# Expert feed-forward: tokens sorted by expert into 16 full tiles instead of 23 padded ones

## The chip, the cores and the metric

One core of a Trainium2 chip runs the whole kernel. The metric is device time in microseconds (us). Three runs of the kernel before took 903.69 to 904.23 us, median 903.89.

## The reference, cut to what matters

Two attention blocks come first (relative-bias attention over 2 x 1024 tokens of 128 features, then a second attention over the same tokens). The change touches only the last block, a mixture of experts in which every token goes to exactly one of 8 experts:

```python
def _moe_mlp(x, gate_w, gate_b, w1, w2):
    xf = x.reshape(b * n, d)                       # 2048 tokens x 128
    logits = xf @ gate_w + gate_b                  # 8 experts
    one_hot = jax.nn.one_hot(jnp.argmax(logits, axis=-1), E, dtype=xf.dtype)
    h = jax.nn.gelu(jnp.einsum('td,edh->teh', xf, w1), approximate=True)   # 128 -> 512
    y = jnp.einsum('teh,ehd->ted', h, w2)                                  # 512 -> 128
    out = jnp.einsum('te,ted->td', one_hot, y)
    return out.reshape(b, n, d)
...
x = x + _moe_mlp(_layernorm(x, ln2_w, ln2_b), gate_w, gate_b, w1, w2)
```

A layer norm of the result is then added to the residual stream.

## The kernel before

Everything until about 805 us of the span is attention, and the change leaves it alone. What follows, in the order of the program:

- **Gate and plan.** VectorE (DVE) picks each token's expert (L1121 to L1134). TensorE (PE) counts, by matmuls over the one-hot matrix, each token's rank within its expert and each expert's total (L1468 to L1473). From these DVE works out a slot for every token (L1140 to L1158). Each expert begins at a fresh tile of 128 slots, so that up to NS = (T - E) // 128 + E = 23 tiles can be needed for T = 2048 tokens, and 23 are always run. Two numbers per token, multiplied by PE with a matrix of places (L1477), are turned into the list of tokens per slot: `gather_u` for reading, `token_u` for writing (empty slots write into a spare region of `moe_out`), and `expert_u`, the expert of each tile (L1163 to L1175). These small steps follow one another through `chain`, which waits for each to end.
- **Gather.** GpSimd (POOL) issues 23 indirect DMAs that read 128 token rows each from `tokens` in DRAM (L797). The rows have been stored there by one DMA per half of the tokens (L556).
- **Tile loop.** For tile j, PE transposes the rows (`sorted_rows`, L1486), DVE applies scale and shift of the layer norm on the way out of PSUM (`features`, L1195), PE multiplies by the expert's first weights (`up`, 8 recorded matmuls, L1494), ScalarE (ACT) applies GELU (L942), PE multiplies by the second weights (`down`, L1503), and DVE copies the result to `slot_y` (`result`, L1188). The weights of the tile's expert are copied by DVE from `w_moe` into one of four buffers (`weights`, L1184). Which expert it is stands in SBUF, so a `value_load` (L1181) brings it into a register of DVE first. PE's order per step is transpose of j+1, up of j, down of j-1, and DVE's is features of j+1, weights of j+2, result of j-1.
- **Scatter.** After its 23 gathers POOL issues 23 indirect DMAs that write the result rows to `moe_out` (L803), each when its tile's result is there.
- **End.** When all have landed, SP loads `moe_out` back in token order (L613), and DVE, POOL and ACT add, normalise, add the residual and store.

The loops of DVE and PE, and POOL's list:

```python
for j in range(NS):                       # DVE, L1201
    if j + 1 < NS: features(j + 1)
    if j + 2 < NS: weights(j + 2)
    if j: result(j - 1)
...
for j in range(NS):                       # PE, L1508
    if j + 1 < NS: sorted_rows(j + 1)
    up(j)
    if j: down(j - 1)
...
for j in range(NS):                       # POOL, L801
    pool.wait_ge(y_ready, j + 1)
    ...
```

## Time and profile before

| | |
|---|---|
| median of 3 runs | 903.89 us (903.69 to 904.23) |
| the profiled execution, its own time | 904.78 us |
| its span in the profile | 902.4 us |
| busy: PE, DVE, ACT, POOL | 802.4, 751.3, 636.4, 242.4 us |
| mean granted clock of PE | 0.948 of full speed |

The profile gives, for one execution, busy times of the engines, groups of instructions by line, and the chain of waits that ended last. Times of rows are microseconds from the start of the span. A row of a timeline has the start, the duration, the engine, the line, the operation, what it writes and reads, and in brackets how long the engine sat idle before it and what ended that. A name with q (DVEq, SPq) is the sequencer of the engine, which handles register loads, register arithmetic and DMA issues and runs ahead of the engine itself. "issue" means that the engine waited for nothing that the profile shows. The groups of rows below come from these views.

### The profile page before, as it was taken

The numbers are of one execution on the slowest core, as the hardware profiler recorded it, in microseconds if no ns is written. First come the engines' busy times: TensorE is split into PE (matmuls) and PEld (weight loads), VectorE is DVE, ScalarE is ACT, GpSimd is POOL, SyncE is SP. The second block draws the span as 40 slices with busy tenths as digits, with TensorE's granted clock in tenths as the row PEclk, the third lists the DMA queues.
The fourth block names the chain that finished last, engine by engine and source line by source line (L and its number), as shares of the span: only waits on it lengthen the run. The fifth ranks groups of instructions, "written<-read, shape, count | busy, mean of one in ns | idle before, by whom it ended". The sixth has DMA issues, their size and how long they took to land.

```text
span 902.4 us, 24156 instructions
## 1 busy us (share of the span) xinstructions
PE 802.4 (89%) x9661; PEld 308.1 (34%) x9661; DVE 751.3 (83%) x1195; ACT 636.4 (71%) x1267; POOL 242.4 (27%) x548
## 2 busy tenths in 40 slices
PE   5279999999999999999999999999999999955950
PEld 3013334333333333343333223322332322344950
DVE  4489988999999998889999998899999999236634
ACT  5037777777776777777778989999989999921311
POOL 3110413200000415232300543332011401004773
PEclk9559999999999999999999999999999999976985
DMA  3665444555555455346313333332321221101313
GB/s 88 185 194 176 144 138 161 170 177 172 171 176 175 137 165 171 117 158 202 108 50 110 107 112 101 102 92 76 93 66 55 61 81 53 31 16 50 51 53 99
DMA packets 69476, 104.78 MB, mean 116 GB/s; under 512 B 15845, under 2 KB 45861, under 8 KB 69365
## 3 DMA queue, kind: packets, MB, share of 16 engines
q1 hardware_dynamic: 62773, 68.30, 26.5%
q10 hardware_dynamic: 5120, 31.94, 9.9%
q0 software_dynamic: 1472, 3.02, 1.6%
q8 instruction: 76, 1.25, 0.6%
q14 instruction: 35, 0.29, 0.1%
HBM read 84.19 MB, written 18.87 MB: 114 GB/s over the span
## 4 chain that ended last, share of the span: by engine, by line
PE 69%; DVE 9%; POOL 6%; issue 4%; DMA 4%; ACT 4%; SPq 3%; POOLq 0%; DVEq 0%
PE bank L1304 23%; PE bank L1323 21%; PE bank L1330 12%; PE bank L1284 7%; DVE unit_max L1013 4%; ACT prob_mem L907 4%; POOL prob_mem L797 3%; POOL moe_out L803 2%; PE bank L1249 1%; DVE stats L956 1%; PE bank L1371 1%; DMA maxima_rows<-max_rows 1%; PE bank L1257 1%; DMA k_parts<-prob_mem 1%; DMA bias_parts<-prob_mem 1%
## 5 line engine op out<-in xcount | busy, mean ns | idle before, releaser
L907 ACT ACTIVATE prob_mem<-bank 128x512 f32<-128x512 f32 x1024 | 556.6, 597 | 137.8 <-PE bank L1330 115.1
L1284 PE MATMUL bank<-k_rows,q_rows 56*128 56x512 bf16 x1024 | 328.2, 392 | 22.2 <-DMA k_rows<-k_parts 12.7
L1323 PE MATMUL bank<-q_rows,k_rows 59*128 59x512 bf16 x1024 | 334.4, 385 | 5.4 <-DMA q_rows<-maxima_rows 1.9
L1009 DVE CUSTOM_DVE_ANT_1 no_use<-bank,w_moe 128x1024 bf16<-128x1024 f32 x256 | 305.6, 1219 | 30.8 <-PE bank L1284 27.7
L1304 PE MATMUL bank<-prob_mem,v_ring 128*32 128x256 f32 x4096 | 320.4, 386 | 7.8 <-issue 6.7
L1013 DVE TENSOR_REDUCE unit_max<-bank 128x1 f32<-128x1024 f32 x256 | 297.4, 1217 | 15.0 <-PE bank L1284 13.4
L1323 PEld LDWEIGHTS bank<-q_rows,k_rows 59*128 59x128 bf16 x1024 | 81.1, 93 | 243.2 <-ACT prob_mem L907 117.9
L708 POOL CAST max_parts<-unit_max 128x8 bf16<-128x8 f32 x64 | 12.1, 189 | 553.3 <-DVE unit_max L1009 312.8
L1304 PEld LDWEIGHTS bank<-prob_mem,v_ring 128*32 128x32 f32 x4096 | 102.6, 109 | 153.6 <-ACT prob_mem L907 60.5
L1330 PE MATMUL bank<-skew_mem,pick 96*32 96x512 bf16 x1664 | 138.3, 390 | 0.0
L1284 PEld LDWEIGHTS bank<-k_rows,q_rows 56*128 56x128 bf16 x1024 | 77.1, 93 | 32.7 <-DVE unit_max L1009 14.7
L1020 DVE TENSOR_TENSOR bank<-bank,w_moe 128x512 f32<-128x512 f32 x96 | 67.0, 698 | 23.1 <-PE bank L1323 23.0
L1330 PEld LDWEIGHTS bank<-skew_mem,pick 96*32 96x32 bf16 x1664 | 29.1, 94 | 71.2 <-issue 71.2
L942 ACT ACTIVATE prob_mem<-bank 128x512 f32<-128x512 f32 x23 | 13.7, 598 | 39.1 <-PE bank L1494 37.8
L859 ACT COPY max_rows<-bank 24x128 bf16<-24x128 bf16 x64 | 15.8, 247 | 24.2 <-PE bank L1313 24.2
L797 POOL DMA_INDIRECT prob_mem<-tokens,gather_u x23 | 23.9, 1037 | 19.5 <-DVE gather_u L1166 12.8
L1494 PE MATMUL bank<-prob_mem 128*128 128x128 f32 x184 | 26.0, 288 | 0.0
L803 POOL DMA_INDIRECT moe_out<-prob_mem,token_u x23 | 23.4, 1019 | 7.0 <-issue 7.0
L852 ACT COPY o_ring<-bank 128x256 f32<-128x256 f32 x64 | 24.3, 380 | 1.2 <-PE bank L1304 1.2
L1503 PE MATMUL bank<-prob_mem 128*128 128x128 f32 x184 | 24.3, 276 | 0.0
L1494 PEld LDWEIGHTS bank<-prob_mem 128*128 128x128 f32 x184 | 24.1, 204 | 0.0
L1024 DVE RECIPROCAL recip<-bank 128x128 f32<-128x128 f32 (+1 forms) x5 | 4.0, 792 | 22.9 <-PE bank L1336 22.9
(181 smaller groups left out, 532.2 us busy)
## 6 DMA issues: line engine op xcount, KB each, us to landing
w_moe<-bias_rows ACTq DMA_DIRECT2D x31, 960.0 KB, 5.8
q_rows<-q_parts SPq DMA_DIRECT2D x252, 48.0 KB
k_rows<-k_parts SPq DMA_DIRECT2D x126, 96.0 KB
skew_mem<-bias_parts SPq DMA_DIRECT2D x32, 378.0 KB, 4.1
unit_sums<-o_ring SPq DMA_DIRECT2D x63, 128.0 KB, 2.3
w_moe<-in_L_ffn_w_dram SPq DMA_DIRECT2D x16, 256.0 KB, 3.0
q_parts<-prob_mem SPq DMA_DIRECT2D x8, 384.0 KB, 3.1
k_parts<-prob_mem SPq DMA_DIRECT2D x24, 128.0 KB, 2.7
```

What stands on the lines that cost most here:

```text
L797: nc.gpsimd.indirect_dma_start(out=slot_rows[:, j, :], out_offset=None, in_=tokens_dram, in_offset=bass.IndirectOffsetOnAxis(ap=gather_u[: ...
L803: nc.gpsimd.indirect_dma_start(out=moe_dram, out_offset=bass.IndirectOffsetOnAxis(ap=token_u[:, j:j + 1], axis=0), in_=slot_y[:, j, :], in ...
L852: nc.scalar.copy(o_ring[:, n % 2, :], AV).then_inc(o_ready, 1)
L907: nc.scalar.activation(prob[:, kb, half * N:(half + 1) * N], b_bank(("exp", exp_no(n, kb, half))), ACT.Exp).then_inc(exp_done, 1)
L1009: nc.vector.tensor_tensor_reduce(out=no_use[:, qb % 2, :].rearrange("p (k c) -> p k c", k=QB), in0=scores.rearrange("p (k c) -> p k c", k= ...
L1013: nc.vector.tensor_reduce(unit_max[:, m % 2, qb:qb + 1], scores, AX.X, ALU.max).then_inc(max_done, 1)
L1020: nc.vector.tensor_tensor(half, half, bias_tab[:, n % 4, at:at + N], ALU.add).then_inc(bias_added, 1)
L1284: return nc.tensor.matmul(sa_slot(QB * m + qb)[:, f, :], q_rows[rows, m % SLOTS, qb * P:(qb + 1) * P], k_rows[rows, m % SLOTS, f * N:(f + ...
L1304: ins = nc.tensor.matmul(AV[VM * c:VM * (c + 1), :], v_ring[:, n % 4, kb, :], prob[:, kb, c * W:(c + 1) * W], start=(kb == 0), stop=(kb == ...
L1323: return nc.tensor.matmul(b_bank(("exp", exp_no(n, kb, f))), k_rows[rows, n % SLOTS, kb * P:(kb + 1) * P], q_rows[rows, n % SLOTS, f * N:( ...
L1330: ins = nc.tensor.matmul(b_bank(("exp", exp_no(n, kb, f)))[32 * c:32 * (c + 1), :], pick[:], skew[0:96, n % 3, at:at + N], start=False, st ...
L1494: ins = nc.tensor.matmul(bank[:, 2 + j % 2, c * P:(c + 1) * P], w_ring[:, j % 4, c * P:(c + 1) * P], slot_feat[:, j % 4, :], start=True, s ...
```

## The change

The tokens are sorted by expert without gaps, so that 16 tiles hold all of them. A tile then may hold tokens of several experts: the tile loop runs over 23 pairs of one tile and one expert (16 tiles and at most 7 borders between experts). For each pair the whole tile goes through the expert, and the result is added to the tile's row of `slot_y` under a mask `in_pair` that is 1 for the rows of that expert. `slot_y` is zeroed first by POOL. Gathers and scatters are 16 each. The scatter of tile j waits for j + 8 results, or for all 23. Scale and shift of the layer norm move to ACT (`tile_features`), once per tile, into `tile_feat`; `features(j)` on DVE is now a copy from the pair's tile, whose number comes by a `value_load` of `tile_u`. So does the row of `slot_y` in `result(j)`.

The diff, cut to its core (declarations, renamed sizes and the repeated NS to TT replacements are left out):

```diff
             store_tokens(1, LN_TAIL)
-            sp.wait_ge(y_scattered, 16 * NS)
+            sp.wait_ge(y_scattered, 16 * TT)
             moe_tiles = moe_dram[0:T].rearrange("(t p) d -> p t d", p=P)
             for g in range(G):
...
@@ -792,14 +800,14 @@
             pool.wait_ge(tokens_stored, 16 * B)
-            pool.wait_ge(gather_known, 1)
-            for j in range(NS):
+            nc.gpsimd.memset(slot_y[:], 0.0).then_inc(y_zeroed, 1)
+            pool.wait_ge(tokens_known, 1)
+            for j in range(TT):
                 nc.gpsimd.indirect_dma_start(out=slot_rows[:, j, :], out_offset=None, in_=tokens_dram,
-                                             in_offset=bass.IndirectOffsetOnAxis(ap=gather_u[:, j:j + 1], axis=0)
+                                             in_offset=bass.IndirectOffsetOnAxis(ap=token_u[:, j:j + 1], axis=0)
                                              ).then_inc(slots_loaded[arrival(j)[0]], 16)
-            pool.wait_ge(tokens_known, 1)
-            for j in range(NS):
-                pool.wait_ge(y_ready, j + 1)
+            for j in range(TT):
+                pool.wait_ge(y_ready, min(j + E, NS))
                 nc.gpsimd.indirect_dma_start(out=moe_dram, out_offset=bass.IndirectOffsetOnAxis(ap=token_u[:, j:j + 1], axis=0),
                                              in_=slot_y[:, j, :], in_offset=None).then_inc(y_scattered, 16)
             for g in range(1, G, 2):
@@ -935,7 +943,15 @@
             act.wait_ge(gate_step, AT_LEAST_STEP)
             nc.scalar.activation(numbers[:, :, 0, :], at_least[:], ACT.Identity, scale=row_no[:, 0:1]).then_inc(numbers_ready, 1)
+            def tile_features(t):
+                act.wait_ge(slot_t_mm, t + 1)
+                nc.scalar.activation(tile_feat[:, t, :], bank[:, t % 2, 0:P], ACT.Identity, scale=ln_par[:, 2:3],
+                                     bias=ln_par[:, 3:4]).then_inc(feat_ready, 1)
+
+            tile_features(0)
             for j in range(NS):
+                if j + 1 < TT:
+                    tile_features(j + 1)
                 act.wait_ge(up_mm, j + 1)
                 if j >= 2:
                     act.wait_ge(down_mm, j - 1)
@@ -1137,43 +1153,38 @@
             dve.wait_ge(rank_mm, 1)
             rank = bank[:, 6, 0:(TT + 1) * E].rearrange("p (t e) -> p t e", e=E)
-            chain(nc.vector.tensor_copy(end_tile[:], rank[:, TT, :].rearrange("p (e o) -> p e o", o=1)))
-            chain(nc.vector.tensor_tensor(counts[:], spread_ap(end_tile[:, :, :], [1, E], [0, TT]),
-                                          spread_ap(tile_start[:, :], [0, E], [1, TT]), ALU.is_gt))
-            chain(nc.vector.tensor_reduce(tiles_of[:], counts[:], AX.X, ALU.add))
-            chain(nc.vector.tensor_tensor(pairs_ef[:], lower[:], spread_ap(tiles_of[:, :, :], [0, E], [1, E]), ALU.mult))
-            chain(nc.vector.tensor_reduce(first_tile[:], pairs_ef[:], AX.X, ALU.add))
-
-            chain(nc.vector.scalar_tensor_tensor(place[:], spread_ap(first_tile[:, :, :], [0, TT], [1, E]), float(P),
-                                                 rank[:, 0:TT, :], ALU.mult, ALU.add))
+            chain(nc.vector.tensor_copy(expert_count[:], rank[:, TT, :].rearrange("p (e o) -> p e o", o=1)))
+            chain(nc.vector.tensor_tensor(pairs_ef[:], lower[:], spread_ap(expert_count[:, :, :], [0, E], [1, E]), ALU.mult))
+            chain(nc.vector.tensor_reduce(first_slot[:], pairs_ef[:], AX.X, ALU.add))
+            chain(nc.vector.tensor_tensor(place[:], spread_ap(first_slot[:, :, :], [0, TT], [1, E]), rank[:, 0:TT, :], ALU.add))
             chain(nc.vector.tensor_tensor(place[:], place[:], hot, ALU.mult))
             chain(nc.vector.tensor_reduce(slot_f[:], place[:], AX.X, ALU.add))
-            slot_by_tile = spread_ap(slot_f[:, :], [1, TT], [0, NS + 1])
-            chain(nc.vector.tensor_tensor(at_least[:], slot_by_tile, spread_ap(tile_start[:, :], [0, TT], [1, NS + 1]), ALU.is_ge))
-            chain(nc.vector.tensor_reduce(slot_tile[:], at_least[:, :, 1:NS + 1], AX.X, ALU.add))
+            slot_by_tile = spread_ap(slot_f[:, :], [1, TT], [0, TT + 1])
+            chain(nc.vector.tensor_tensor(at_least[:], slot_by_tile, spread_ap(tile_start[:, :], [0, TT], [1, TT + 1]), ALU.is_ge))
+            chain(nc.vector.tensor_reduce(slot_tile[:], at_least[:, :, 1:TT + 1], AX.X, ALU.add))
             chain(nc.vector.scalar_tensor_tensor(place_in_tile[:], slot_tile[:], -float(P), slot_f[:], ALU.mult, ALU.add))
             nc.vector.tensor_tensor(has_place, spread_ap(col_no[:, :], [0, TT], [1, P]),
                                     spread_ap(place_in_tile[:, :], [1, TT], [0, P]), ALU.is_equal).then_inc(numbers_ready, 1)
-            nc.vector.tensor_tensor(numbers[:, :, 1, :], at_least[:], spread_ap(next_tile_no[:, :], [1, TT], [0, NS + 1]),
+            nc.vector.tensor_tensor(numbers[:, :, 1, :], at_least[:], spread_ap(next_tile_no[:, :], [1, TT], [0, TT + 1]),
                                     ALU.mult).then_inc(numbers_ready, 1)
+            chain(nc.vector.tensor_tensor(counts[:], spread_ap(first_slot[:, :, :], [1, E], [0, TT]),
+                                          spread_ap(tile_start[:, :], [0, E], [1, TT]), ALU.is_ge))
+            chain(nc.vector.tensor_reduce(tiles_of[:], counts[:], AX.X, ALU.add))
             dve.wait_ge(numbers_mm, 1)
-            chain(nc.vector.tensor_copy(slot_sum[:], bank[:, 7, 0:NS + 1]))
-            chain(nc.vector.scalar_tensor_tensor(slot_sum[:], bank[:, 7, NS + 1:2 * NS + 2], float(P), slot_sum[:], ALU.mult, ALU.add))
-            chain(nc.vector.tensor_tensor(slot_token[:], slot_sum[:, 0:NS], slot_sum[:, 1:NS + 1], ALU.subtract))
-            nc.vector.tensor_scalar(gather_u[:], slot_token[:], -float(P), 0.0, ALU.add, ALU.max).then_inc(gather_known, 1)
-            chain(nc.vector.scalar_tensor_tensor(unused[:], slot_token[:], 0.0, spare_no[:], ALU.is_le, ALU.mult))
-            nc.vector.scalar_tensor_tensor(token_u[:], slot_token[:], -float(P), unused[:], ALU.add, ALU.add).then_inc(tokens_known, 1)
-
-            chain(nc.vector.tensor_tensor(end_tile[:], first_tile[:], tiles_of[:], ALU.add))
-            chain(nc.vector.tensor_tensor(ended[:], spread_ap(end_tile[:, :, :], [0, NS], [1, E]),
-                                          spread_ap(tile_no[:, :], [1, NS], [0, E]), ALU.is_le))
+            chain(nc.vector.tensor_copy(slot_sum[:], bank[:, 7, 0:TT + 1]))
+            chain(nc.vector.scalar_tensor_tensor(slot_sum[:], bank[:, 7, TT + 1:2 * TT + 2], float(P), slot_sum[:], ALU.mult, ALU.add))
+            chain(nc.vector.tensor_tensor(slot_token[:], slot_sum[:, 0:TT], slot_sum[:, 1:TT + 1], ALU.subtract))
+            nc.vector.tensor_scalar(token_u[:], slot_token[:], -float(P), None, ALU.add).then_inc(tokens_known, 1)
+
+            chain(nc.vector.tensor_tensor(ended[:], spread_ap(tiles_of[:, :, :], [0, NS], [1, E]), turn_no[:], ALU.is_le))
             chain(nc.vector.tensor_reduce(expert_f[:], ended[:], AX.X, ALU.add))
-            chain(nc.vector.tensor_scalar(expert_f[:], expert_f[:], float(E - 1), None, ALU.min))
-            nc.vector.tensor_copy(expert_u[:], expert_f[:]).then_inc(expert_known, 1)
-            dve.wait_ge(expert_known, 1)
+            nc.vector.tensor_scalar(expert_u[:], expert_f[:], -1.0, None, ALU.add).then_inc(expert_known, 1)
+            chain(nc.vector.tensor_tensor(tile_f[:], pair_no[:], expert_f[:], ALU.subtract))
+            nc.vector.tensor_copy(tile_u[:], tile_f[:]).then_inc(expert_known, 1)
+            dve.wait_ge(expert_known, 2)
             dve.wait_ge(moe_loaded, 16 * 2 * E)
             def weights(j):
@@ -1184,20 +1195,36 @@
                 nc.vector.tensor_copy(w_ring[:, j % 4, :], w_moe[:, bass.ds(e, 1), :].rearrange("p o w -> p (o w)")).then_inc(w_ready, 1)
             def result(j):
+                tile = dve.value_load(tile_u[0:1, j:j + 1], min_val=0, max_val=TT - 1)
                 dve.wait_ge(down_mm, j + 1)
-                nc.vector.tensor_copy(slot_y[:, j, :], bank[:, 4 + j % 2, 0:D]).then_inc(y_ready, 1)
+                if j:
+                    dve.wait_ge(y_ready, j)
+                rows = slot_y[:, bass.ds(tile, 1), :].rearrange("p o d -> p (o d)")
+                nc.vector.scalar_tensor_tensor(rows, bank[:, 4 + j % 2, 0:D], in_pair[:, j:j + 1], rows, ALU.mult,
+                                               ALU.add).then_inc(y_ready, 1)
             def features(j):
-                dve.wait_ge(slot_t_mm, j + 1)
+                tile = dve.value_load(tile_u[0:1, j:j + 1], min_val=0, max_val=TT - 1)
+                dve.wait_ge(feat_ready, min(j, TT - 1) + 1)
                 if j >= 4:
                     dve.wait_ge(up_mm, j - 3)
-                nc.vector.tensor_scalar(slot_feat[:, j % 4, :], bank[:, j % 2, 0:P], ln_par[:, 2:3], ln_par[:, 3:4],
-                                        ALU.mult, ALU.add).then_inc(slot_t_ready, 1)
+                nc.vector.tensor_copy(slot_feat[:, j % 4, :], tile_feat[:, bass.ds(tile, 1), :].rearrange("p o n -> p (o n)")
+                                      ).then_inc(slot_t_ready, 1)
             weights(0)
             weights(1)
             features(0)
+
+            chain(nc.vector.tensor_tensor(ended[:], ended[:], spread_ap(first_slot[:, :, :], [0, NS], [1, E]), ALU.mult))
+            chain(nc.vector.tensor_reduce(pair_start[:, 0:NS], ended[:], AX.X, ALU.max))
+            chain(nc.vector.scalar_tensor_tensor(pair_start[:, 0:NS], tile_f[:], float(P), pair_start[:, 0:NS], ALU.mult, ALU.max))
+            chain(nc.vector.tensor_scalar(pair_slot[:], tile_f[:], float(P), row_no[:, 0:1], ALU.mult, ALU.add))
+            chain(nc.vector.tensor_tensor(from_next[:], pair_slot[:], pair_start[:, 1:NS + 1], ALU.is_ge))
+            chain(nc.vector.tensor_tensor(in_pair[:], pair_slot[:], pair_start[:, 0:NS], ALU.is_ge))
+            chain(nc.vector.tensor_tensor(in_pair[:], in_pair[:], from_next[:], ALU.subtract))
+            dve.wait_ge(y_zeroed, 1)
+
             for j in range(NS):
                 if j + 1 < NS:
                     features(j + 1)
...
@@ -1482,7 +1509,7 @@
                 pe.wait_ge(slots_loaded[arrival(j)[0]], 16 * arrival(j)[1])
                 if j >= 2:
-                    pe.wait_ge(slot_t_ready, j - 1)
+                    pe.wait_ge(feat_ready, j - 1)
                 nc.tensor.transpose(bank[:, j % 2, 0:P], slot_rows[:, j, :], ident[:]).then_inc(slot_t_mm, 1)
             def up(j):
@@ -1506,7 +1533,7 @@
             sorted_rows(0)
             for j in range(NS):
-                if j + 1 < NS:
+                if j + 1 < TT:
                     sorted_rows(j + 1)
                 up(j)
                 if j:
```

On DVE one step of the tile loop read as follows before (the loop of L1201; `expert_u` is the list of experts, L1184 the copy of the weights, L1188 the result, L1195 the features):

```order
L1181 TENSOR_LOAD expert_u
L1181 ISA x2
L1184 ISA [waits down_mm]
L1184 COPY prob_mem<-w_moe 128x1024
L1188 COPY prob_mem<-bank 128x128 [waits down_mm]
L1195 TENSOR_SCALAR prob_mem<-bank,ln_par 128x128 [waits up_mm,slot_t_mm]
```

and now so (`tile_u` is the list of tiles; L1195 is now the copy of the weights, L1203 the result, L1212 the features):

```order
L1192 TENSOR_LOAD expert_u
L1192 ISA x2
L1195 ISA [waits down_mm]
L1195 COPY prob_mem<-w_moe 128x1024
L1198 TENSOR_LOAD tile_u
L1198 ISA x2
L1203 ISA [waits y_ready,down_mm]
L1203 SCALAR_TENSOR_TENSOR prob_mem<-bank,in_pair,prob_mem 128x128
L1208 TENSOR_LOAD tile_u
L1208 ISA x2
L1212 ISA [waits up_mm,feat_ready]
L1212 COPY prob_mem<-prob_mem 128x128
```

Each of the three instructions of a step now has its own register load and register arithmetic ahead of it, where one of three had before.

Between the first features and the second, DVE now works out the masks:

```order
L1212 COPY prob_mem<-prob_mem 128x128
L1219 TENSOR_TENSOR ended<-ended,first_slot 128x184
L1220 TENSOR_REDUCE pair_start<-ended 128x23 [waits gate_step]
L1221 SCALAR_TENSOR_TENSOR pair_start<-tile_f,pair_start 128x23 [waits gate_step]
L1222 TENSOR_SCALAR pair_slot<-tile_f,row_no 128x23 [waits gate_step]
L1223 TENSOR_TENSOR from_next<-pair_slot,pair_start 128x23 [waits gate_step]
L1224 TENSOR_TENSOR in_pair<-pair_slot,pair_start 128x23 [waits gate_step]
L1225 TENSOR_TENSOR in_pair<-in_pair,from_next 128x23 [waits gate_step]
L1208 TENSOR_LOAD tile_u [waits y_zeroed,gate_step]
L1208 ISA x2
L1212 ISA [waits feat_ready]
```

Seven chained steps now stand there, where nothing stood before; the second features come behind them.

On ACT the table load of GELU stood right behind `numbers`, and now stands behind the features of two tiles (L948):

```order
L944 ACTIVATE numbers<-prob_mem,row_no 128x16x17 [waits gate_step]
L948 ACTIVATE prob_mem<-bank,ln_par 128x128 [waits slot_t_mm] x2
L958 ACT_TABLE_LOAD
L958 ACTIVATE prob_mem<-bank 128x512 [waits up_mm]
L948 ACTIVATE prob_mem<-bank,ln_par 128x128 [waits slot_t_mm]
```

The table load moved past two waits for PE's transposes.

## Rows read from the trace of the kernel before

**Rows 1.** Busy time of each engine by stretch (PE, PEld, DVE, ACT, POOL, PEclk, DMA, GB/s).

```profile
840.00:850.00 10.00, 10.00 (x92) 10.00 (x91) 6.93 (x16) 3.21 (x6) 7.72 (x8) 1.00 0.30 46
...
870.00:880.00 10.00, 0.43 (x4) 0.24 (x3) 0.29 (x1) 0.00 (x0) 7.56 (x9) 0.66 0.16 52
```

**Rows 2.** Timeline of POOL, first gather, first and last scatter.

```profile
820.63 1.24 POOL L797 DMA_INDIRECT prob_mem<-tokens,gather_u  x1 [12.75 <-DVE gather_u L1166]
...
851.49 1.01 POOL L803 DMA_INDIRECT moe_out<-prob_mem,token_u  x1 [0.30 <-issue]
...
880.66 0.97 POOL L803 DMA_INDIRECT moe_out<-prob_mem,token_u  x1 [0.30 <-issue]
```

**Rows 3.** Timeline of PE, start of the tile loop and one step of it.

```profile
824.72 0.47 PE L1486 MATMUL bank<-ident,prob_mem 128*128 128x128 f32 x1 [0.77 <-DMA prob_mem<-tokens,gather_u]
824.99 1.92 PE L1494 MATMUL bank<-prob_mem 128*128 128x128 f32 x8
...
829.72 1.06 PE L1494 MATMUL bank<-prob_mem 128*128 128x128 f32 x8
...
831.62 1.06 PE L1494 MATMUL bank<-prob_mem 128*128 128x128 f32 x8
```

**Rows 4.** Timeline of DVE in the tile loop, and its last result.

```profile
825.24 0.41 DVE L1195 TENSOR_SCALAR prob_mem<-bank,ln_par 128x128 f32<-128x128 f32 x1 [0.83 <-PE bank L1486]
825.97 0.69 DVE L1184 COPY prob_mem<-w_moe 128x1024 f32 x1 [0.32 <-issue]
...
829.81 0.29 DVE L1188 COPY prob_mem<-bank 128x128 f32<-128x128 f32 x1 [1.23 <-PE bank L1503]
830.02 0.40 DVE L1195 TENSOR_SCALAR prob_mem<-bank,ln_par 128x128 f32<-128x128 f32 x1
830.68 0.69 DVE L1184 COPY prob_mem<-w_moe 128x1024 f32 x1 [0.25 <-issue]
...
870.47 0.29 DVE L1188 COPY prob_mem<-bank 128x128 f32<-128x128 f32 x1 [0.66 <-PE bank L1503]
```

**Rows 5.** Instructions of lines L1181 and L1184 in DVE's sequencer (min/median/max ns).

```profile
L1181 DVEq TENSOR_LOAD <-expert_u x23: 301/304/550, 821.4 to 864.1; - x23
L1181 DVEq FUSED_REGOPS  x23: 190/190/207, 821.9 to 864.4; - x23
...
L1184 DVEq FUSED_REGOPS  x23: 57/57/65, 822.2 to 864.7; - x23
```

**Rows 6.** Timeline of DVE in the plan, and the first two copies of weights.

```profile
811.74 0.29 DVE L1141 TENSOR_TENSOR counts<-end_tile,tile_start 128x128 f32<-128x128 f32 x1
...
813.87 0.56 DVE L1153 TENSOR_TENSOR prob_mem<-slot_f,tile_start 128x384 f32<-128x384 f32 x1
...
819.57 0.18 DVE L1166 TENSOR_SCALAR gather_u<-slot_token 128x23 uint32<-128x23 f32 x1
...
820.16 0.35 DVE L1171 TENSOR_TENSOR ended<-end_tile,tile_no 128x184 f32<-128x184 f32 x1
...
822.36 1.44 DVE L1184 COPY prob_mem<-w_moe 128x1024 f32 x2 [1.04 <-issue]
```

**Rows 7.** Groups of instructions by line: a memset of POOL, a copy of ACT.

```profile
L676 POOL MEMSET v_ring<- 128x1024 f32 x1 | 1.0, 951 | 0.0
...
L852 ACT COPY o_ring<-bank 128x256 f32<-128x256 f32 x64 | 24.3, 380 | 1.2 <-PE bank L1304 1.2
```

**Rows 8.** Second store of the tokens on SP; DMA issues (KB each, us to landing).

```profile
811.39 0.40 SPq L556 DMA_DIRECT2D tokens<-norm  x1
...
tokens<-norm SPq DMA_DIRECT2D x2, 512.0 KB, 3.2
```

**Rows 9.** Busy time of PE by stretch (PE busy, PEclk, DMA, GB/s).

```profile
600.00:620.00 20.00, 18.67 (x202) 1.00 0.37 101
...
790.00:795.00 5.00, 1.07 (x16) 0.97 0.17 49
795.00:800.00 5.00, 4.63 (x23) 0.50 0.00 0
```

50 lines of the change are left out of this document (29 added, 21 removed).

## The prediction

> **What bounds the kernel now.** I read the busy times by stretch first, for the part behind 820 us. At 840 to 850 us both PE and POOL are at work all the time (POOL shows 7.72 of 10 us, the rest being the issue gaps between its DMAs), and at 870 to 880 us POOL alone still works [rows 1]. The timeline of POOL says what this is. The first gather begins at 820.63 us, the first scatter at 851.49 and the last of 23 scatters at 880.66, with nothing but 0.30 us of issue ahead of each [rows 2]. So 23 gathers take 30.9 us, 1.34 us each, and the scatters stand (880.66 - 851.49) / 22 = 1.33 us apart. The timelines of the two other engines show that they have finished long before. One step of the tile loop takes PE 831.62 - 829.72 = 1.90 us [rows 3], and DVE's last result is there at 870.47 + 0.29 = 870.8 us [rows 4]. The end of the span hangs on POOL's list, which is 10 us late against the last result. Everything behind the last scatter waits for it and isn't changed.
>
> **What the change does, part by part.**
>
> *POOL's list* loses 14 of 46 DMAs, 14 x 1.33 = 18.7 us. Only a part of it can be had, since the tile loop still has 23 steps and the last scatter needs the last result. The question is when that result comes.
>
> *The plan* ahead of the gathers gets shorter. Two operations on 128 elements per partition leave the chain (the one whose row stands there takes 0.29 us and, with the gap behind it, 0.32), and come back behind `numbers`, where DVE waits for PE anyway: 0.64 us. Three operations of 384 elements become 272 wide. Between 128 elements (0.29 us) and 384 (0.56 us) one element costs 1.05 ns, so each gives 0.12 us: 0.36. Together the token list is known 1.0 us earlier, and the first gather begins at 819.6 instead of 820.63; it begins 0.9 us behind the end of the instruction that makes the list, 819.57 + 0.18 [rows 2, 6]. The list of experts loses three small operations and gains two, so it comes about 1.2 us earlier, ahead of need.
>
> *The memset on POOL* is new: twice the size of one that took 0.95 us, so 1.9 us [rows 7]. The tokens' store is issued at 811.39 us and lands 3.2 us behind its issue of 0.4 us [rows 8], at 815.0. The memset is over at 816.9, and POOL waits for the token list until 818.8. It costs nothing; uncovered it would cost at most its 1.9 us.
>
> *The start of the loop.* PE's first `up` waited for the second gather (its transpose at 824.72, `up` at 824.99) [rows 3], so it begins at 824.0. Features now go PE, ACT, DVE. On ACT a copy of 256 elements from PSUM takes 0.38 us [rows 7], so 0.3 for 128; this lies under the wait for the second gather. ACT's table load stands now behind two of these, between them and the first GELU, and that GELU waits for `up(0)`, which takes 1.92 us at the clock of that time [rows 3]. I cost it at nothing, with 0.3 us as its upper bound.
>
> *The masks* are seven chained operations on DVE between the first features and the second. Two are 184 wide, 0.35 us and a gap [rows 6], the others 23 wide at some 0.21 from start to start (the 0.18 of the 23-wide row and a gap). That makes 2 x 0.38 + 5 x 0.21 = 1.8 us. With the first features done at 823.7 they end at 825.5. A register load that follows such a chain took 1.04 us from the last operation to the copy [rows 6], so the second features start at 826.5 and `up(1)` at 826.75. Before it was 824.99 + 1.92 = 826.9. **The microsecond won in the plan is lost again.** Bounds: 0.8 us of the 1.04 if its load had been a fast one, which would leave a gain of 0.4.
>
> *DVE's step* decides. One step had one register load, now it has three. In DVE's sequencer a load takes 0.304 us, the register arithmetic behind it 0.19 and 0.057 [rows 5]. From the start of an instruction to the start of one with a load ahead of it it is 825.97 - 825.24 = 0.73 us, and 830.68 - 830.02 = 0.66 where the earlier one had been handed over before its engine was free [rows 4]. The sequencer runs ahead: two copies of weights, the second with its own load, take 1.44 us together, thus 0.72 each and hardly more than the copy's own 0.69 [rows 6, 4]. So a load hides behind the instruction ahead of it, but not behind another load. Three of them give a step of 3 x 0.72 = 2.16 us on DVE, where PE needs 1.90. The work itself hides in it: 0.69 for weights, under 0.4 for a copy of features and some 0.3 for the result. **The loop changes from PE-bound to DVE-bound.** Bounds for one load: 0.55 (the sequencer's own parts, where nothing else cost anything; PE's 1.90 then holds) and 0.80 (0.73 and a gap of 0.07 for the additional wait in `result`).
>
> *The sum.* `result(0)` comes at 829.9, as before (829.81) [rows 4], since the low clock holds PE back there. `result(19)` follows 19 x 2.16 = 41.0 us later, at 870.9. Features of step 22 follow 0.7 later, at 871.6 and done at 871.8. Then PE has `up(22)`, `down(21)`, `down(22)`, each half of 1.90: 874.65. The result is written by 875.0. POOL's gathers end at 819.6 + 16 x 1.34 = 841.1; its scatter j waits for result j + 7, which come 2.16 us apart against 1.33 for a scatter, so POOL waits for each, and the last goes out right behind the last result. With the 0.9 us that POOL took from the token list to its first gather it starts at 875.9, where it was 880.66 [rows 2]. **That is 4.8 us less.** The profiled execution, 904.78, becomes 900.0. It lies 0.9 above the median of 903.89, which becomes **899.1**. With the bounds of one load, 0.01 us on each of 57 loads is 0.57 us: 0.80 gives 903.7, and the lower bound the first rival below.
>
> About 0.2% (1.8 us) is what a measurement of this kernel can tell from no change.
>
> **The rivals.**
>
> 1. *The loop stays PE-bound.* Loads overlap with each other's arithmetic or cost less than 0.63 each, so a step stays at 1.90. Then the last result comes as before less 0.15, is written at 870.6, and the last scatter starts at 871.5: 9.2 us less, 894.7. For it speaks that the sequencer's own parts sum to 0.55 us [rows 5]; against it that no pair of rows is closer than 0.66. I give it 0.17.
>
> 2. *Loads are dearer than that, and the kernel gets slower.* A DVE step above (4.8 / 19) + 2.16 = 2.41 us, or 0.80 a load, takes the gain away. One of the 23 loads took 0.55 us instead of 0.304 [rows 5]. If all did, a step would be 3 x (0.72 + 0.25) = 2.9 us and the time 899.1 + 19 x 0.74 = 913. Against it: 0.304 is the median of 23, and the slow one is the first, behind a wait. 0.07.
> The Trainium skill, "DMA: Bandwidth & Descriptors", section "Latency and other measured facts", gives such a load a floor of about 600 ns. By that rule a step would be above 3 us and the kernel slower by more than 10 us; the trace's 0.304 us disagrees, and I go by the trace.
>
> 3. *PE's clock falls.* In a DVE-bound loop PE stands still for 0.26 of 2.16 us in each step, 12%. At the low clock `up` takes 1.92 us instead of 0.95 [rows 3], a step 3.9, that is 1.7 us more than DVE's; three such steps take the gain, ten make it 911. Against it: PE was 93% busy at 600 to 620 us and had full clock throughout; the clock fell only behind a stretch with PE busy for 1.07 of 5 us [rows 9]. 88% is much nearer to the first. 0.04.
> The Trainium skill, "TensorE: Matmul & The Clock Gate", section "A second HAM failure mode: psum-queue depth-cycling", describes a kernel in which micro-idles between groups of matmuls made the clock oscillate; by that rule this rival would be the outcome. No row here shows small idles doing it.
>
> 4. *The gain drowns.* Twice as many sequencer instructions in the loop, fetched late a few times, and a load price near 0.78 leave less than 1.8 us. 0.10.
>
> **How the numbers follow.** DVE-bound as summed 0.62, PE-bound 0.17, drowned 0.10, dear loads 0.07, clock 0.04. The likeliest gives 899.1, with 896.5 to 902 as its own range. To hold 8 in 10 the range must take in the PE-bound case at 894.7, with the 0.4 us that the masks may leave and as much for the start of the loop, and reach to the upper bound of the load: 893.9 to 903.7. Faster by over 0.2% is the first two, 0.79, and no more; within 0.2% 0.11 and slower 0.10.
>
> **What would show it.** Right: in the timeline of DVE the starts of `result` stand 2.1 to 2.25 us apart, with idle "issue" time ahead of each instruction and none put down to PE; PE shows gaps of 0.2 to 0.3 us in each step that end with the features; the first gather begins at 819.6, the first scatter waits for DVE, and the last starts within 1 us of the last result, near 876 us. A second `up` before 826.3 or after 827.2 makes the price of the masks wrong. Results 1.90 us apart speak for rival 1, above 2.4 for rival 2; a granted clock below 1.00 between 832 and 870 us for rival 3. The whole argument is wrong if the last scatter starts later than 1.5 us behind the last result.

## The result, and the profile after

The changed kernel is a little slower. Over 20 runs each its median is 905.68 us against 903.74, a ratio of 1.0024 with a 95% interval of 1.0016 to 1.0032. The forecast was 899.1, in a range of 893.9 to 903.7; the time lies above it.

The profiled execution of the changed kernel took 905.70 us, with a span of 903.7. The first lines of its page, and busy times by stretch (PE, PEld, DVE, ACT, POOL, PEclk, DMA, GB/s), as in [rows 1]:

```profile
span 903.7 us, 24350 instructions
...
PE 805.6 (89%) x9654; PEld 308.6 (34%) x9654; DVE 751.2 (83%) x1200; ACT 643.7 (71%) x1283; POOL 230.3 (25%) x536
...
840.00:850.00 10.00, 8.53 (x68) 7.69 (x68) 5.30 (x13) 4.40 (x9) 1.44 (x2) 1.00 0.03 8
870.00:880.00 10.00, 8.13 (x66) 7.67 (x67) 4.39 (x11) 2.39 (x4) 4.39 (x5) 1.00 0.08 27
```

At 840 to 850 us PE was at work for all 10 us before and is now for 8.53. POOL's part fell from 7.72 to 1.44, and at 870 to 880 us, where POOL alone worked before, the loop is still running. Now the timeline of POOL, for [rows 2] and the memset of [rows 7]:

```profile
813.17 1.80 POOL L803 MEMSET prob_mem<- 128x2048 f32 x1 [6.78 <-DMA tokens<-norm]
817.43 1.24 POOL L806 DMA_INDIRECT prob_mem<-tokens,token_u  x1 [2.46 <-DVE token_u L1180]
...
837.67 0.95 POOL L806 DMA_INDIRECT prob_mem<-tokens,token_u  x1 [0.30 <-issue]
...
847.11 1.01 POOL L811 DMA_INDIRECT moe_out<-prob_mem,token_u  x1 [8.49 <-DVE prob_mem L1203]
...
880.75 0.97 POOL L811 DMA_INDIRECT moe_out<-prob_mem,token_u  x1 [0.68 <-DVE prob_mem L1203]
882.02 0.97 POOL L811 DMA_INDIRECT moe_out<-prob_mem,token_u  x1 [0.30 <-issue]
```

The 16 gathers are over at 838.6 us, POOL then stands still for 8.49 us, and from there each scatter but the last waits for a result of DVE. POOL is no longer what bounds the block. DVE's timeline shows what does. The first row is the one operation that begins the gate in both kernels (L1137, before L1121); L1212 is `features`, L1195 `weights`, L1203 `result`:

```profile
804.42 0.23 DVE L1137 TENSOR_TENSOR gate_mean<-meanvar,gate_const 128x64 f32<-128x64 f32 x1
...
823.30 0.18 DVE L1225 TENSOR_TENSOR in_pair<-in_pair,from_next 128x23 f32<-128x23 f32 x1
824.30 0.23 DVE L1212 COPY prob_mem<-prob_mem 128x128 f32 x1 [0.81 <-DVE in_pair L1225]
...
828.60 0.35 DVE L1203 SCALAR_TENSOR_TENSOR prob_mem<-bank,in_pair,prob_mem 128x128 f32 x1 [1.33 <-PE bank L1530]
...
846.48 0.35 DVE L1203 SCALAR_TENSOR_TENSOR prob_mem<-bank,in_pair,prob_mem 128x128 f32 x1
847.32 0.23 DVE L1212 COPY prob_mem<-prob_mem 128x128 f32 x1 [0.49 <-issue]
848.08 0.69 DVE L1195 COPY prob_mem<-w_moe 128x1024 f32 x1 [0.54 <-issue]
848.93 0.35 DVE L1203 SCALAR_TENSOR_TENSOR prob_mem<-bank,in_pair,prob_mem 128x128 f32 x1 [0.16 <-issue]
...
853.00 0.69 DVE L1195 COPY prob_mem<-w_moe 128x1024 f32 x1 [0.54 <-issue]
854.30 0.35 DVE L1203 SCALAR_TENSOR_TENSOR prob_mem<-bank,in_pair,prob_mem 128x128 f32 x1 [0.61 <-issue]
...
881.07 0.35 DVE L1203 SCALAR_TENSOR_TENSOR prob_mem<-bank,in_pair,prob_mem 128x128 f32 x1 [0.60 <-PE bank L1530]
```

A step now takes 848.93 - 846.48 = 2.45 us: 0.84 from `result` to `features`, 0.76 to `weights`, 0.85 to `result`. DVE is idle ahead of each one, with "issue", not with a wait for PE. Its engine rests while its sequencer loads:

```profile
L1198 DVEq TENSOR_LOAD <-tile_u x23: 299/302/410, 826.6 to 880.1; - x23
L1198 DVEq FUSED_REGOPS  x23: 190/190/190, 826.9 to 880.5; - x23
L1203 DVEq FUSED_REGOPS  x23: 69/69/69, 828.5 to 881.0; - x23
L1195 DVEq FUSED_REGOPS  x23: 57/65/65, 819.2 to 875.8; - x23
```

PE waits in its turn, 0.3 us in each step, and not at a lower clock:

```profile
824.67 2.05 PE L1521 MATMUL bank<-prob_mem 128*128 128x128 f32 x8 [0.56 <-DVE prob_mem L1212]
...
847.65 1.13 PE L1521 MATMUL bank<-prob_mem 128*128 128x128 f32 x8 [0.31 <-issue]
850.10 1.13 PE L1521 MATMUL bank<-prob_mem 128*128 128x128 f32 x8 [0.32 <-issue]
```

That holds for the steady part of the loop. Its start ran at the low clock for longer than before, which the experiment e7 takes up.

To compare executions one needs a common start, since what stands ahead of the block ended up to 3.75 us apart in the executions profiled here. I count from the first operation of the gate. Before it stood at

```profile
805.91 0.23 DVE L1121 TENSOR_TENSOR gate_mean<-meanvar,gate_const 128x64 f32<-128x64 f32 x1
```

From there to the start of the last result it was 870.47 - 805.91 = 64.56 us and is 76.65; to the last scatter it was 74.75 and is 77.60, which is 2.85 us more. From the last scatter to the end of the span it was 21.74 and is 21.68.

### The profile page after: what moved, and what is told of

It reads as the page before. It is cut to its first block, busy times and chain, and to the rows that moved or that the text cites. A ratio compares the mean times of both kernels' runs of the same rounds, so it can differ in the third digit from the quotient of the medians.

```text
span 903.7 us, 24350 instructions
## 1 busy us (share of the span) xinstructions
PE 805.6 (89%) x9654; PEld 308.6 (34%) x9654; DVE 751.2 (83%) x1200; ACT 643.7 (71%) x1283; POOL 230.3 (25%) x536
## 4 chain that ended last, share of the span: by engine, by line
PE 74%; DVE 9%; DMA 4%; ACT 4%; issue 4%; SPq 2%; POOL 1%; POOLq 0%; DVEq 0%
PE bank L1331 23%; PE bank L1350 21%; PE bank L1357 12%; PE bank L1311 7%; DVE unit_max L1029 4%; ACT prob_mem L915 4%; PE bank L1521 3%; PE bank L1530 2%; PE bank L1276 1%; DMA maxima_rows<-max_rows 1%; DVE stats L972 1%; PE bank L1398 1%; PE bank L1284 1%; DMA bias_parts<-prob_mem 1%; POOL rstd L660 1%
## 5 line engine op out<-in xcount | busy, mean ns | idle before, releaser
L1521 PE MATMUL bank<-prob_mem 128*128 128x128 f32 x184 | 28.3, 302 | 8.0 <-issue 7.4
L1521 PEld LDWEIGHTS bank<-prob_mem 128*128 128x128 f32 x184 | 24.8, 209 | 11.7 <-issue 11.7
L1195 DVE COPY prob_mem<-w_moe 128x1024 f32 x23 | 16.5, 717 | 12.2 <-issue 12.2
L1530 PE MATMUL bank<-prob_mem 128*128 128x128 f32 x184 | 25.1, 282 | 0.0
L1530 PEld LDWEIGHTS bank<-prob_mem 128*128 128x128 f32 x184 | 23.4, 199 | 0.0
L1040 DVE RECIPROCAL recip<-bank 128x128 f32<-128x128 f32 (+1 forms) x5 | 4.0, 793 | 22.9 <-PE bank L1363 22.9
```

Source lines behind the costliest of these rows:

```text
L1195: nc.vector.tensor_copy(w_ring[:, j % 4, :], w_moe[:, bass.ds(e, 1), :].rearrange("p o w -> p (o w)")).then_inc(w_ready, 1)
L1521: ins = nc.tensor.matmul(bank[:, 2 + j % 2, c * P:(c + 1) * P], w_ring[:, j % 4, c * P:(c + 1) * P], slot_feat[:, j % 4, :], start=True, s ...
L1530: ins = nc.tensor.matmul(bank[:, 4 + j % 2, 0:D], hidden[:, j % 2, c, :], w_ring[:, j % 4, HID + c * D:HID + (c + 1) * D], start=(c == 0), ...
```

## The experiments

Two theories stood against each other at first, and the expectations name a third, "hop": that the features' new way over ACT is what makes the step long. **A: register loads.** The step is the sum of what DVE's sequencer does for its three loads and their addresses. **B: the work itself.** The masked addition is slower than a plain copy, or reads the PSUM bank and SBUF in a way that delays its neighbours. Questions on the masks, on the waits, and on what POOL's list was worth alone came up on the way. All comparisons go by the ratio to the kernel before on the same chip; its median was 902.73 us for the four runs e1, e2, e4 and e8, 903.03 for e3, e5, e7 and e9, 903.18 for the last three. "Step" is the median distance of DVE's results. The ratio is taken over all runs of both kernels and can differ by up to 0.2% from the quotient of the two medians.

| run | step | gate to last result | gate to last scatter | median us | ratio (95%) |
|---|---|---|---|---|---|
| before | 1.90 | 64.56 | 74.75 | 903.74 | |
| after | 2.45 | 76.65 | 77.60 | 905.68 | 1.0024 (1.0016 to 1.0032) |
| e1, two loads | 1.85 | 65.47 | 66.42 | 893.36 | 0.9901 (0.9881 to 0.9921) |
| e2, two loads, the other one out | 1.80 | 63.00 | 63.95 | 891.67 | 0.9894 (0.9867 to 0.9922) |
| e3, one load | 1.81 | 62.69 | 63.64 | 892.55 | 0.9886 (0.9866 to 0.9906) |
| e4, four loads | 3.06 | 88.86 | 89.49 | 918.35 | 1.0166 (1.0145 to 1.0188) |
| e8, three loads, plain copy | 2.45 | 76.64 | 77.53 | 905.46 | 1.0030 (1.0017 to 1.0042) |
| e5, before with three loads | 2.13 | 68.85 | 76.54 | 905.47 | 1.0027 (1.0016 to 1.0038) |
| e9, one wait fewer | 2.38 | 75.35 | 76.30 | 905.11 | 1.0023 (1.0013 to 1.0033) |
| e7, two loads, masks late | 1.84 | 63.52 | 64.47 | 892.82 | 0.9886 (0.9868 to 0.9904) |
| e10, e7 and e9 together | 1.81 | 63.29 | 64.24 | 892.56 | 0.9872 (0.9832 to 0.9911) |
| e11, before, 16 DMAs | 1.90 | 64.28 | 65.17 | 897.07 | 0.9939 (0.9915 to 0.9963) |
| e12, before, small weights | 1.90 | 64.67 | 72.48 | 901.35 | 0.9973 (0.9956 to 0.9990) |

### e1: two loads instead of three

The result of a pair takes the register that its features loaded; everything is still computed.

```diff
             def result(j):
-                tile = dve.value_load(tile_u[0:1, j:j + 1], min_val=0, max_val=TT - 1)
+                tile = tile_of[j]
...
             def features(j):
-                tile = dve.value_load(tile_u[0:1, j:j + 1], min_val=0, max_val=TT - 1)
+                tile = tile_of[j] = dve.value_load(tile_u[0:1, j:j + 1], min_val=0, max_val=TT - 1)
```

> Two register loads per step instead of three: result(j) uses the register that features(j) has loaded; all computation stays. Theory (loads): the step of DVE is the sum of its sequencer's work, 0.81 us for each load with its instruction. Two loads and a short dispatch give 1.8, below PE's 1.90, so the step falls from 2.44 to 1.90 us, the last result comes some 11 us earlier and the time is 894 to 896 us, below both kernels. Rival (engine): the step is long because result reads and adds slot_y and waits for the result before it; then the step stays near 2.4 and the time at 905.7. Rival (hop): the step is long because features now pass ACT; unchanged here too, 905.7.

The kernel becomes 1.0% faster than before. DVE's timeline, where `weights` is L1195, `result` L1205 and `features` L1214:

```profile
844.41 0.23 DVE L1214 COPY prob_mem<-prob_mem 128x128 f32 x1
845.17 0.69 DVE L1195 COPY prob_mem<-w_moe 128x1024 f32 x1 [0.54 <-issue]
845.78 0.34 DVE L1205 SCALAR_TENSOR_TENSOR prob_mem<-bank,in_pair,prob_mem 128x128 f32 x1
846.32 0.23 DVE L1214 COPY prob_mem<-prob_mem 128x128 f32 x1 [0.19 <-PE bank L1523]
```

The result follows the copy of weights after 0.61 us, where it was 0.85. Its own load is gone. The load of the features is done ahead of time, while the weights are copied: they follow the result by 0.54 us, and what they wait for is PE. The step is PE's again. The way over ACT is unchanged, so theory "hop" falls here as well.

### e2 and e3: fixed tiles

```diff
             def features(j):
-                tile = dve.value_load(tile_u[0:1, j:j + 1], min_val=0, max_val=TT - 1)
...
-                nc.vector.tensor_copy(slot_feat[:, j % 4, :], tile_feat[:, bass.ds(tile, 1), :].rearrange("p o n -> p (o n)")
+                nc.vector.tensor_copy(slot_feat[:, j % 4, :], tile_feat[:, min(j, TT - 1), :]
```

> features(j) copies from tile min(j, 15), known when the kernel is built, so it has no load; the pair's features are then the wrong tile's. The way over ACT, the waits and result stay. Theory (loads): two loads left, step 1.90, 894 to 896 us, like the run with the shared register. Rival (hop): nothing of the hop is removed, 905.7. Rival (engine): 905.7.

e3 does the same for the result as well, with a fixed row `slot_y[:, j * TT // NS, :]`:

> Neither features nor result has a load: both take a tile known when the kernel is built, so that one load per step is left, as before the change; features and sums then belong partly to the wrong tiles. Theory (loads): with one load DVE needs 0.81 and two short dispatches, and PE's 1.90 holds the step, so the time is that of two loads, 892 to 895 us, and not lower. If instead every load on its own costs time on the path, one load less must give another 10 us (882).

e2 has a step of 1.80 us and e3 one of 1.81. The second load taken away gives nothing measurable in the times (0.9894 and 0.9886, intervals on top of each other; one of e2's seven runs took 899.79 us, which widens its interval), since PE bounds the step by then. In the traces both end 2.5 to 2.8 us ahead of e1, and that comes mostly from the start of the loop: their second `up` doesn't wait for the masks (see e7). PE's own step is 1.79 us where it has no transpose, in the pairs from 16 on, and 1.90 where it has one.

### e4: a fourth load

```diff
             def result(j):
                 tile = dve.value_load(tile_u[0:1, j:j + 1], min_val=0, max_val=TT - 1)
+                dve.value_load(tile_u[0:1, j:j + 1], min_val=0, max_val=TT - 1)
```

> A fourth load per step, of the same tile number, unused, ahead of the one in result. Theory (loads): load and its arithmetic take 0.30 + 0.19 + 0.02 us, with gaps 0.55, so the step goes from 2.44 to 3.0 and the time up by 21 x 0.55 = 11.6 to about 917. Rivals (engine, hop): the sequencer has slack, and the time stays within 1 us of 905.7.

One more load, whose value nobody uses, makes the block 11.9 us longer and the kernel 1.66% slower than before. DVE's timeline (`result` is L1204, `features` L1213 here):

```profile
846.79 0.23 DVE L1213 COPY prob_mem<-prob_mem 128x128 f32 x1 [0.49 <-ACT prob_mem L948]
847.55 0.69 DVE L1195 COPY prob_mem<-w_moe 128x1024 f32 x1 [0.53 <-issue]
849.00 0.35 DVE L1204 SCALAR_TENSOR_TENSOR prob_mem<-bank,in_pair,prob_mem 128x128 f32 x1 [0.75 <-issue]
849.84 0.23 DVE L1213 COPY prob_mem<-prob_mem 128x128 f32 x1 [0.49 <-ACT prob_mem L948]
```

From weights to result it is now 1.45 us instead of 0.84, while the two other distances are 0.84 and 0.76 as before. The idle time named after ACT in `features` is the same 0.49 that stands with "issue" elsewhere. So an added load costs 0.61 us, undiluted: 3.06 - 2.45. Steps of 1.8, 2.45 and 3.06 us for two, three and four loads are the line of theory A, with PE's step as its floor.

### e8: the same loads, less work

The masked addition becomes a plain copy, which leaves mask and sum out:

```diff
-                nc.vector.scalar_tensor_tensor(rows, bank[:, 4 + j % 2, 0:D], in_pair[:, j:j + 1], rows, ALU.mult,
-                                               ALU.add).then_inc(y_ready, 1)
+                nc.vector.tensor_copy(rows, bank[:, 4 + j % 2, 0:D]).then_inc(y_ready, 1)
```

> result(j) writes slot_y by a plain copy instead of multiply and add (the mask and the sum over pairs are left out); its load and its waits stay. Theory (loads): the step stays at 2.44 and the time at 905 to 906. Rival (engine): reading slot_y and the two-input operation cost time in every step, and the time falls by several us.

```profile
845.98 0.29 DVE L1203 COPY prob_mem<-bank 128x128 f32 x1
846.82 0.23 DVE L1211 COPY prob_mem<-prob_mem 128x128 f32 x1 [0.54 <-issue]
847.58 0.69 DVE L1195 COPY prob_mem<-w_moe 128x1024 f32 x1 [0.54 <-issue]
848.42 0.29 DVE L1203 COPY prob_mem<-bank 128x128 f32 x1
```

The operation takes 0.29 us instead of 0.35 and the step stays at 2.44 to 2.45: 0.84, 0.76, 0.84. What it saves goes into the idle time behind it, 0.54 instead of 0.49. Theory B falls.

### e5: the loads alone, on the kernel before

```diff
             def result(j):
+                dve.value_load(expert_u[0:1, j:j + 1], min_val=0, max_val=E - 1)
...
             def features(j):
+                dve.value_load(expert_u[0:1, j:j + 1], min_val=0, max_val=E - 1)
```

> The kernel before with two more loads per step, of the expert's number, unused, ahead of features and result. Theory (loads): the step of DVE becomes 2.1 to 2.4 us, and the last result comes 5 to 10 us later, but POOL's list of 46 DMAs ended 10 us behind the last result, so the time stays within 0.3% of before. If the loads are dear only together with the change's own operations, the step stays at 1.90.

Here the step is 2.13 us, close to the 2.16 of the forecast and not 2.45. In this kernel neither `result` (L1189) nor `features` (L1197) has an address that comes from a register. DVE's timeline:

```profile
844.56 0.69 DVE L1184 COPY prob_mem<-w_moe 128x1024 f32 x1 [0.34 <-PE bank L1505]
845.22 0.29 DVE L1189 COPY prob_mem<-bank 128x128 f32<-128x128 f32 x1
845.93 0.41 DVE L1197 TENSOR_SCALAR prob_mem<-bank,ln_par 128x128 f32<-128x128 f32 x1 [0.43 <-PE bank L1496]
846.70 0.69 DVE L1184 COPY prob_mem<-w_moe 128x1024 f32 x1 [0.36 <-PE bank L1505]
```

From weights to result it is 0.66 us, to features 0.71, to weights 0.77. In the changed kernel these are 0.84, 0.84 and 0.76. The copy of weights, whose address comes from a register in both kernels, stands as far behind its predecessor in both. The two others are dearer by 0.18 and 0.13 where their addresses come from a register; `result` has got a second wait as well, `features` had two before. The loads alone thus come near to what I had put on them in sum, and the rest of the 0.3 us comes with using what they bring.

That the kernel got 0.27% slower was not due to the step. The last result starts at 873.30 us and the last scatter at 880.99, 7.7 us behind it, so POOL bounds the end as it did before, and still its list takes longer: 61.8 us from the first gather to the last scatter where it was 60.0. Its gathers, all of them with min/median/max in ns, and three of them in the timeline of POOL:

```profile
L797 POOL DMA_INDIRECT prob_mem<-tokens,gather_u x23: 940/1117/1310, 819.2 to 849.9; - x23
```

```profile
844.26 1.12 POOL L797 DMA_INDIRECT prob_mem<-tokens,gather_u  x1 [0.30 <-issue]
845.68 0.94 POOL L797 DMA_INDIRECT prob_mem<-tokens,gather_u  x1 [0.30 <-issue]
846.93 1.28 POOL L797 DMA_INDIRECT prob_mem<-tokens,gather_u  x1 [0.30 <-issue]
```

The copies of weights near them are those at 844.56 and 846.70 above. The gather in the middle has no copy of weights beside it and takes 0.94 us. The one ahead of it has a whole copy inside it and takes 1.12, the one behind begins in the middle of a copy and takes 1.28. That the copies do it is a reading of these rows so far; the next run tests it.

### e12: is it the copy of weights?

The kernel before with weights copied in full for the first four tiles and 8 elements wide from there, which leaves those tiles' own weights out:

```diff
-                nc.vector.tensor_copy(w_ring[:, j % 4, :], ...
+                width = WE if j < 4 else 8
+                nc.vector.tensor_copy(w_ring[:, j % 4, 0:width], ...
```

> The kernel before with the weights copied whole for the first four tiles and only 8 of 1024 columns for the others (later tiles then use old weights). POOL's DMAs are untouched, but 19 of DVE's 0.69 us copies are gone. In e5_before_three_loads more gathers took 1.1 to 1.3 us instead of 0.94 than before, and its end came 1.8 us later, though POOL issued the same list. If gathers and scatters are held up by DVE's copies running beside them, all but the first few now take 0.94 to 0.97, and POOL's list of 60.0 us gets 2 to 3 us shorter, about 901. If their length is their own, nothing changes.

```profile
L797 POOL DMA_INDIRECT prob_mem<-tokens,gather_u x23: 940/944/1381, 819.9 to 848.3; - x23
```

Behind the first five the gathers take 0.94 to 0.95 us each, POOL's list is 57.8 us long instead of 60.0, and the kernel is 0.27% faster than before. The loop's step stays 1.90. So a part of POOL's 1.33 us per DMA in the kernel before was DVE's copy. The Trainium skill, "SBUF — State Buffer", section "🔬 SBUF: two separate sides", says that GpSimd cannot write the descriptors of its DMA while DVE copies fp32 within SBUF, and is held up for the whole of that instruction. The direction agrees with the traces. The size agrees where a gather begins inside a running copy: in the traces of the kernel before and of e5 all 14 such gathers end 0.81 to 0.83 us behind the end of the copy (the one at 846.93 at 848.21, the copy at 847.39). It doesn't where the copy begins later. One that starts 0.3 to 0.5 us into a gather lets it end 0.12 to 0.13 us behind the copy, so the gather at 844.26, with the whole 0.69 us copy inside it, has only 0.18 us more. One that starts 0.03 to 0.13 us into a gather costs it nothing: 7 gathers, all of 0.94 us.

### e9: one wait less on the features

```diff
             def features(j):
-                dve.wait_ge(feat_ready, min(j, TT - 1) + 1)
-                if j >= 4:
+                if j < TT:
+                    dve.wait_ge(feat_ready, j + 1)
+                else:
```

> The changed kernel with one wait instead of two ahead of each features: the wait for up is left out up to step 15, since a result waited for before implies it, and the wait for the tile's features behind step 15, where it has been met. Everything is computed as in the changed kernel. Theory (loads): features follow the result by 0.76 us as the copy of weights with its one wait does, instead of 0.84; the step falls by 0.08 to 2.36, the time by 21 x 0.08 = 1.7 us to about 904. If the 0.08 belongs to the operation and not to the second wait, nothing changes.

```profile
845.43 0.35 DVE L1203 SCALAR_TENSOR_TENSOR prob_mem<-bank,in_pair,prob_mem 128x128 f32 x1
846.20 0.23 DVE L1213 COPY prob_mem<-prob_mem 128x128 f32 x1 [0.42 <-issue]
846.97 0.70 DVE L1195 COPY prob_mem<-w_moe 128x1024 f32 x1 [0.54 <-issue]
```

From result to features it is 0.77 us instead of 0.84, and the step is 2.38 instead of 2.45. From the gate to the last scatter the trace has 1.3 us less; in the times it can't be told from the changed kernel (1.0023 against 1.0024). A second wait on `features`, whose address comes from a register, costs 0.07 us on this path. The second wait of `result` wasn't taken away in any run.

### e7 and e10: masks behind the start

e7 is e1 with the seven mask operations moved into the loop:

```diff
+                if j == 0:
+                    masks()
                 if j:
                     result(j - 1)
```

> The shared register of the run e1_share, and the seven operations for the masks moved behind the second features and the third weights, ahead of the first result, which is the first to need a mask. All is computed. Theory: up(1) no longer waits for the masks (0.56 to 0.75 us of PE idle), and the loop, now held by PE, starts that much earlier: 0.6 to 1 us below e1_share, 892 to 893 us. If the masks hid under the low clock of PE anyway, it is the same as e1_share.

```profile
820.66 1.91 PE L1526 MATMUL bank<-prob_mem 128*128 128x128 f32 x8
822.58 1.91 PE L1526 MATMUL bank<-prob_mem 128*128 128x128 f32 x8
...
826.21 1.13 PE L1526 MATMUL bank<-prob_mem 128*128 128x128 f32 x8
```

The second `up` follows the first without a gap; with the masks ahead of the second features it waited 0.56 us (above, 824.67). From the gate to the last scatter it is 64.47 us instead of e1's 66.42. The times, 892.82 and 893.36, have intervals that overlap, so the gain of the late masks is shown by the trace alone.

The gap of 0.56 us is only a part of these 1.95. The third `up` took 1.13 us here and 1.92 in e1, where it stands at

```profile
827.08 1.92 PE L1523 MATMUL bank<-prob_mem 128*128 128x128 f32 x8
```

PE's granted clock stays at 0.50, its low level (1.2 GHz), until 829 us in e1, 25.9 us behind the gate, and until 826 us in e7, 22.9 us behind it. All profiled executions fall in one of two groups. In the five whose PE waited 0.55 to 0.62 us ahead of its second `up` (the changed kernel, e1, e4, e8, e9) the clock rises between 25.5 and 26.5 us behind the gate; in the other eight, PE at work without a gap there, between 21.5 and 23.5. e1 and e7 differ in the place of the masks alone. e10 has this and e9's edit together:

> The shared register, the late masks and the one wait ahead of each features together; everything is computed. Theory: PE now holds the step (1.90 with a transpose, 1.79 without), so taking 0.08 from DVE's step gives little: 892 us, up to 1 us below e7_share_late, 1.2% below the kernel before and 1.4% below the changed one.

It computes everything and is 1.3% faster than before (0.9872, 0.9832 to 0.9911), some 1.5% faster than the change as made. It has the shortest block of the versions that compute everything, by 0.23 us; its time can't be told from that of e7.

### e11: POOL's list alone

What would the shorter list have brought with nothing else changed? The kernel before, with 16 gathers and scatters, whose last seven tiles use the rows of tile 15 and whose `moe_out` is filled by an early copy of `x`, so that the output is another:

```diff
-            for j in range(NS):
-                pool.wait_ge(y_ready, j + 1)
+            for j in range(TT):
+                pool.wait_ge(y_ready, min(j + E, NS))
```

> The kernel before with 16 gathers and 16 scatters, scatter j waiting for j + 8 results as in the change, and nothing else of it; tiles 16 to 22 reuse the rows of tile 15 and their results are left out (moe_out is filled by a copy of x far ahead instead). This is the first half of the change alone. Theory: the last result stays where it was, 64.6 us behind the start of the gate, the last scatter follows it within 1 us instead of 10, and the time falls by 9 us to 894. If something other than POOL's list held the end, it stays above 900.

The last result in the timeline of DVE, then the last two scatters in that of POOL:

```profile
871.13 0.29 DVE L1192 COPY prob_mem<-bank 128x128 f32<-128x128 f32 x1 [0.66 <-PE bank L1508]
```

```profile
870.75 0.97 POOL L807 DMA_INDIRECT moe_out<-prob_mem,token_u  x1 [0.82 <-DVE prob_mem L1192]
872.02 0.97 POOL L807 DMA_INDIRECT moe_out<-prob_mem,token_u  x1 [0.30 <-issue]
```

From the gate to the last scatter it is 65.17 us instead of 74.75: 9.6 us less, and the last scatter starts 0.9 behind the last result. The time fell by 0.6% only, some 5.5 us, where 9 were expected. The ten runs spread from 895.08 to 901.86 us, wider than in the other experiments but e2, and the profiled one, 895.70, is among the short ones. In it the gate began at 806.85 us, 0.9 later than before. Whether the added copy of 1 MB does that, or makes the long runs long, isn't known.

## Why the prediction was wrong

**Right:** the bottleneck and where it would go. POOL's list bounded the block and gave 9.6 us of the trace when shortened alone (e11; the forecast's first rival had 9.2), though only 0.6% of the time. The loop then went from PE to DVE's sequencer, the scatters waited for results, and the last one started right behind the last result. The plan got 1.6 us shorter up to the first copy of weights and 1.7 up to the first gather, where I had 1.2 and 1.0. The memset is hidden with 2.46 us to spare. The masks took the gain of the plan back, as forecast, but by another way than the text had. The second `up` came 20.25 us behind the gate, 826.16 on the forecast's scale, ahead of the 826.3 below which it called its price of the masks wrong. Still `result(0)` wasn't earlier, since PE had waited 0.56 us and its clock rose 3 us later against the gate than in the kernel before. In e3, without that wait, `result(0)` came 22.80 us behind the gate instead of 24.18. That the sum has 24.0 for this term is thus in part luck; e7 shows that the delay was avoidable. ACT's operations for the features take 0.46 us each where I had 0.3, which doesn't show in `result(0)`.

**The step that failed** is "Three of them give a step of 3 x 0.72 = 2.16 us on DVE". From the start of one instruction with a load to the next it is 0.84, 0.76 and 0.84 us there, and the step 2.44 to 2.45. Along the forecast's own sum, from the gate to the last scatter:

| term | predicted | measured | difference |
|---|---|---|---|
| gate to `result(0)` | 829.9 - 805.91 = 24.0 | 24.18 | +0.2 |
| 19 steps | 41.0 | 876.77 - 828.60 = 48.17 | +7.1 |
| to the last result written | 875.0 - 870.9 = 4.1 | 4.65 | +0.55 |
| to the last scatter | 0.9 | 0.60 | -0.3 |
| sum | 70.0 | 77.6 | +7.6 |

Of the 7.1 us, 19 x 0.285 = 5.4 is the size of the usual step. 1.7 is four steps of 2.82 to 2.91 us. The first of them, up to 831.44, has a copy of weights of 0.95 us in it and ends in a wait of 0.34 us for PE. The three others can be seen on DVE as 0.37, 0.46 and 0.37 us more of idle time (at 835.09, 854.30 and 872.64); the rival "The gain drowns" had such late steps in it. What they are isn't settled. Ahead of 854.30 the sequencer's load took 0.41 us, 0.11 more than usual, ahead of 872.64 no more than usual. The gate began 1.5 us earlier in this execution than in that of before, and so the span is 6.1 us above the 897.6 that the sum gives.

Why a load was dearer than 0.72 has two parts. The first is a misreading. The two copies of weights take 1.44 us together, and half of it was taken for the distance of their starts. But the second one ends 0.69 us behind its own start, so the starts stand 1.44 - 0.69 = 0.75 us apart, and three of these are 2.25: 0.09 of the missing 0.285. The copy of weights stood 0.76 to 0.77 behind its predecessor in the changed kernel and in e5 alike. The second part is what the figure, taken from the one instruction with a register address and one wait, doesn't cover. `features` has a second wait, which costs 0.07 (e9). `result` has a second wait too; if it costs the same, an estimate from e9, the two make 0.14. The rest, some 0.05, wasn't tested. In `result` and `features` the register arithmetic ahead takes 69 ns instead of 57 to 65. That e5's step came out at 2.13, near 2.16, doesn't confirm the 0.72: its distances are 0.66, 0.71 and 0.77, and two of its loads feed no address.

**The bound was known and not believed.** The text named 0.80 us per load as the upper bound and as the point at which the gain is gone, with a step of 2.41. It came out at 0.815, with four slow steps on top. The second wait in `result`, which it named only under the bound, was in the code for certain and should have gone into the sum itself, and so should that of `features`. The range ended at the break-even of one term, as if nothing could be added to it, and the chance of slower was put at 0.10 though the margin was 0.08 us a load, 0.25 on a step.

**The rivals.** PE-bound falls with the step. Dear loads, with a chance of 0.07, came true at a smaller size than the 0.25 us that I tried there. The clock stayed at 1.00 in both stretches above, with PE busy for 8.53 and 8.13 of 10 us and a gap in each step. In that rival's sum ten slow steps of 1.7 us each on 899.1 would make 916 and not 911; nothing else used it. The Trainium skill's floor of about 600 ns for such a load ("DMA: Bandwidth & Descriptors", section "Latency and other measured facts") was set aside for the 0.30 us of the row. The row is right for the load alone, with a median of 0.302 us over 23 of them. What a step pays for one more load is 0.61 (e4), since the assertion, the arithmetic and the hand-over come with it. By the page's figure in place of 0.302 the step would be above 3 us, and 2.45 was measured.
